# Four transformer layers on one core: narrow attentions turn queries and keys by DMA, weight loads and buffer releases change places

## What is computed

```python
x = x + L0_xattn(layernorm(x), ctx)   # narrow: 32 heads of 16, 8 key heads, rotary positions
x = x + L0_ffn(layernorm(x))          # 512 -> 1792 -> 512, gated by silu
x = x + L1_xattn(layernorm(x), ctx)   # wide: 32 heads of 128, keys = context + latents, rms norms
x = x + L1_ffn(layernorm(x))          # 8 experts of rank 16, two picked
x = x + L2_xattn(layernorm(x), ctx)   # narrow, no rotary positions
x = x + L2_ffn(layernorm(x))          # 8 experts 512 x 512, two picked
x = x + L3_xattn(layernorm(x), ctx)   # wide, keys = context, additive mask
x = x + L3_ffn(layernorm(x))          # base 512 x 512 and 16 experts of rank 64

# one attention
scores = einsum('bhqd,bhkd->bhqk', q, k) * scale
probs = softmax(scores)
ctx_out = einsum('bhqk,bhkd->bhqd', probs, v)
return ctx_out @ Wo
```

## Time and profile before

| | before |
|---|---|
| median of 3 runs | 2209.41 us (2207.28 to 2210.55) |
| profiled execution | 2211.04 us, its span 2209.2 us |
| PE busy | 2017.0 us (91%) |
| DVE busy | 1607.9 us (73%) |
| ACT busy | 1350.0 us (61%) |
| POOL busy | 206.2 us (9%) |
| DMA, dynamic queue | 142.51 MB, 27.4% of 16 engines' span |

### The profile page before, as it was taken

How to read it: one execution, slowest core, us unless ns; L and a number is a source line. 1 busy time by engine, 2 the same in 40 slices (tenths; PEclk the granted TensorE clock), 3 DMA queues, 4 the chain that set the end, 5 groups by cost and what they waited for, 6 DMA issues and landing times.

```text
span 2209.2 us, 40607 instructions
## 1 busy us (share of the span) xinstructions
PE 2017.0 (91%) x14240; PEld 1161.3 (53%) x14240; DVE 1607.9 (73%) x4139; ACT 1350.0 (61%) x3913; POOL 206.2 (9%) x211
## 2 busy tenths in 40 slices
PE   3898999999999999999975798999899999999788
PEld 2554444465655666666643455444455555555444
DVE  6676555676767777777768667766788888888873
ACT  3665212287777777777753566333688888888621
POOL 3664000000000000000000354000000000000010
PEclk8999999999999999999998999999999999999989
DMA  4000111224444444444440000111133433343200
GB/s 194 21 11 2 58 58 39 77 58 87 105 80 89 80 106 96 80 89 89 92 87 20 20 20 11 68 39 58 28 90 72 89 88 86 65 90 84 61 5 39
DMA packets 268761, 145.10 MB, mean 66 GB/s; under 512 B 259472, under 2 KB 259472, under 8 KB 261136
## 3 DMA queue, kind: packets, MB, share of 16 engines
q1 hardware_dynamic: 268560, 142.51, 27.4%
HBM read 77.44 MB, written 2.10 MB: 36 GB/s over the span
## 4 chain that ended last, share of the span: by engine, by line
PE 73%; DVE 12%; ACT 6%; DMA 4%; issue 4%; POOL 1%; SPq 0%; ACTq 0%; DVEq 0%; POOLq 0%
PE bank L659 67%; DMA pT<-hid 3%; ACT hid L1608 2%; PE bank L770 1%; DVE hid L2220 1%; PE bank L1048 1%; DVE xnT_lo L1793 1%; DVE wa_lo L1726 1%; PE bank L786 1%; PE bank L787 1%; ACT probs L1567 1%; DVE xn L1782 1%; DVE stats L1749 1%; DVE negmax_n L1909 1%; DVE bd_lo L1922 0%
## 5 line engine op out<-in xcount | busy, mean ns | idle before, releaser
L659 PE MATMUL bank<-xnT_hi,wa_hi 128*128 128x512 f16 x736 | 279.8, 380 | 4.5 <-PE bank L659 2.6
L659 PE MATMUL bank<-xnT_lo,wa_hi 128*128 128x512 f16 x736 | 279.7, 380 | 0.0
L659 PE MATMUL bank<-xnT_hi,wa_lo 128*128 128x512 f16 x736 | 279.5, 380 | 0.0
L659 PE MATMUL bank<-wo_hi,oT_hi 128*128 128x512 f16 x576 | 219.9, 382 | 27.7 <-DVE oT_lo L2210 26.7
L2220 DVE SCALAR_TENSOR_TENSOR hid<-probs,inv_total,hid 128x256 f16<-128x256 f32 (+1 forms) x512 | 180.0, 413 | 81.5 <-ACT hid L1608 81.5
L659 PE MATMUL bank<-wo_hi,oT_lo 128*128 128x512 f16 x576 | 219.9, 382 | 0.0
L659 PE MATMUL bank<-wo_lo,oT_hi 128*128 128x512 f16 x576 | 219.9, 382 | 0.0
L659 PE MATMUL bank<-wa_hi,xnT_hi 128*128 128x512 f16 (+3 forms) x640 | 203.7, 324 | 5.5 <-DVE xnT_lo L1793 2.2
L659 PE MATMUL bank<-wa_lo,xnT_hi 128*128 128x512 f16 (+3 forms) x640 | 203.7, 324 | 0.0
L659 PE MATMUL bank<-wa_hi,xnT_lo 128*128 128x512 f16 (+3 forms) x640 | 203.5, 323 | 0.0
L1567 ACT ACTIVATE probs<-bank,negmax,rms_r 128x256 f32<-128x256 f32 x256 | 141.2, 561 | 98.5 <-DVE negmax L2176 98.5
(11 more groups left out here) (260 smaller groups left out, 4973.4 us busy)
## 6 DMA issues: line engine op xcount, KB each, us to landing
raw<-in_w_qkv_dram SPq DMA_DIRECT2D x18, 1536.0 KB, 7.0
raw<-in_w_out_dram SPq DMA_DIRECT2D x18, 1024.0 KB, 5.4
raw<-in_w_ffn_dram SPq DMA_DIRECT2D x15, 1024.0 KB, 4.9
pT<-hid SPq DMA_TRANSPOSE x256, 3.1
raw<-in_w_ffn0d_dram SPq DMA_DIRECT2D x7, 512.0 KB, 3.7
x<-in_x_dram SPq DMA_DIRECT2D x4, 512.0 KB, 5.4
expert_b<-in_expert_b_dram SPq DMA_DIRECT2D x1, 2048.0 KB, 9.5
kT<-k SPq DMA_TRANSPOSE x128, 2.4
```

The lines of the kernel that those rows point to most:

```text
L659: mm = pe.matmul(dst, l, r, start=start and k == 0, stop=stop and k == n - 1)
```

## The change

1. **Narrow attentions.** `turn_q`, `turn_k`, `q_rows` and `k_rows` are gone from PE, ACT and DVE. `turn_narrow(n, b)` on SP issues two transposing DMAs a tile: all 16 blocks of `q_parts` into `qst`, and eight blocks of `k_parts` into `kst`. For the latter `k_parts` is laid out twice as wide (128 x 1024), with the zero blocks in it, so that the turned tile is block-diagonal at once; POOL clears `k_parts` instead of `kst`. `proj_q(b)` on PE waits for the reader of bank Q in place of `nb_kst`. ACT and DVE refill the parts once the DMA has landed.
2. **SP's order.** The loads that stood ahead of each narrow attention are now issued between its tiles (`NARROW_LOADS`) or after them. In the wide stages the loads due in step s stand between `turn_probs(s)` and `turn_keys(s + 2)`, in both layers.
3. **Releases.** In the wide stages the wait and release of `qkv_used` move behind `project_q`, those of `out_used` into the next step behind `project_kv`. In the experts of layer 2 the release moves behind the first matmuls of the next expert; in the feed-forward of layer 0 it moves ahead by one down-projection.

```diff
+            def turn_narrow(n, b):
+
+                BB = n * B + b
+                if b == 0:
+                    sp.wait_ge(n_consts, n + 1)
+                if b >= 2:
+                    sp.wait_ge(ng_turned, (BB - 1) * G)
+                sp.wait_ge(nb_qparts if n == 0 else nb_qlo, b + 1)
+                sp.dma_start_transpose(qst_turned[:, b % 2], q_parts[:, :]).then_inc(nb_qturned, 16)
+                sp.wait_ge(nb_kparts if n == 0 else nb_klo, b + 1)
+                sp.dma_start_transpose(kst_turned[:, b % 2], k_parts[:, :]).then_inc(nb_kturned, 16)
+
+            def narrow(n, last):
+
+                for b in range(B):
+                    turn_narrow(n, b)
+                    if b in NARROW_LOADS[n]:
+                        load_item(NARROW_LOADS[n][b])
+                for k in range(max(NARROW_LOADS[n].values()) + 1, last):
+                    load_item(k)
...
             for n in range(2):
+                narrow(n, FIRST_LOAD[n])
                 turn_keys(n, 0)
                 turn_keys(n, 1)
                 for s in range(UNITS):
                     turn_probs(n, s)
+                    for k in wide_loads(n, s):
+                        load_item(k)
                     if s < UNITS - 2:
                         turn_keys(n, s + 2)
-                    for k in wide_loads(n, s):
-                        load_item(k)
...
-                pool.memset(bd_flat[:, 0:2048], 0.0)
+                pool.memset(k_parts[:, :], 0.0).then_inc(nb_kzero, 1)
...
                     if e == 0:
-                        pe.wait_ge(nb_kst, BB + 1)
-                        pe.wait_ge(nb_qst_b, BB + 1)
+                        pe.wait_ge(nb_vlo, BB + 1)
+                        pe.wait_ge(nb_qturned, 16 * (BB + 1))
+                        pe.wait_ge(nb_kturned, 16 * (BB + 1))
...
-                    if g == 1 and f < B:
-                        turn_q(f, 0)
-                    if g == 2 and f < B:
-                        turn_q(f, 1)
-                        turn_k(f)
...
+                    done = s - LATE[n] - 2
+                    if done >= 0 and done % B == B - 1 and done < UNITS - 1:
+                        pe.wait_ge(w_out, n * UNITS + done + 1)
+                        pe.sem_inc(out_used, 1)
...
+                    if s + 5 < UNITS:
+                        project_q(U, s)
                     if s < UNITS - 2 and (s + 2) % B == B - 1:
                         pe.wait_ge(w_kvproj, U + 3)
                         pe.sem_inc(qkv_used, 1)
-                    if s + 5 < UNITS:
-                        project_q(U, s)
...
-                    if r % B == B - 1:
-                        pe.wait_ge(e_y, r + 1)
+                    if r % B == 0:
+                        pe.wait_ge(e_y, r)
                         pe.sem_inc(qkv_used, 1)
```

More of the change, by code:

```diff
@@ L190 @@
 FIRST_LOAD = [min(t) for t in WIDE_LOADS]
+NARROW_LOADS = [{b: NUMBER[item] + 2 for item, b in t.items()} for t in (
+    {("w_out0", 0): 2, ("w_ffn0", 0): 4}, {("w_out2", 0): 2, ("w_ffn2", 0): 4})]
 def wide_loads(n, s):
@@ L319, in p_turned_part @@
             return pT_flat[:, at:at + HPG * S]
-        k_parts = squares[:, 0:256].bitcast(F16)
-        q_part_slots, k_part_slots = (t.rearrange("p (c m s d) -> p s m c d", m=2, s=4, d=ND) for t in (q_parts, k_parts))
+        k_parts = squares[:, 0:512].bitcast(F16)
+        q_part_slots = q_parts.rearrange("p (c m s d) -> p s m c d", m=2, s=4, d=ND)
+        k_part_slots = k_parts.rearrange("p (c u s d) -> p s u c d", u=4, s=4, d=ND)[:, :, 0:4:3]
         def v_heads(t):
@@ L530, in turn_keys @@
                                        k16[:, u % 2, 0:runs * P]).then_inc(w_kturned[u % 2], 16)
+            for k in range(1, min(NARROW_LOADS[0].values())):
+                load_item(k)
+                if k == 2:
+                    sp.dma_start(expert_b[:, :, :], ins["expert_b"]).then_inc(expert_b_loaded, 16)
+                    sp.dma_start(wgate2[:, :], ins["wgate2"]).then_inc(wgate2_loaded, 16)
             for n in range(2):
+                narrow(n, FIRST_LOAD[n])
                 turn_keys(n, 0)
@@ L536, in _ @@
                     turn_probs(n, s)
+                    for k in wide_loads(n, s):
+                        load_item(k)
                     if s < UNITS - 2:
                         turn_keys(n, s + 2)
-                    for k in wide_loads(n, s):
-                        load_item(k)
                 if n == 0:
-                    for k in range(FIRST_LOAD[0] + len(WIDE_LOADS[0]), FIRST_LOAD[1]):
+                    for k in range(FIRST_LOAD[0] + len(WIDE_LOADS[0]), min(NARROW_LOADS[1].values())):
                         load_item(k)
@@ L724, in proj_kv @@
                         pe.sem_inc(qkv_used, 1)
[L726 to L751, removed]
                 def scores(b, e):
@@ L1226, in ffn2 @@
                     expert(48 + 2 * b)
+                    if b == 0:
+                        pe.wait_ge(e_y, 48)
+                        pe.sem_inc(qkv_used, 1)
                     if b >= 3:
@@ L1362, in k_part @@
                     if b:
-                        act.wait_ge(nb_turn_k, BB)
+                        act.wait_ge(nb_kturned, 16 * BB)
+                    else:
+                        act.wait_ge(nb_kzero, n + 1)
                     if rope:
@@ L1425, in narrow @@
                         k_part(f)
-                    if g == 1 and f < B:
-                        q_rows(f)
                     if g == 6 and f < B:
@@ L1911, in row_max @@
                                       negate=True).then_inc(ng_max, 1)
-                def k_rows(b):
-                    BB = n * B + b
-                    dve.wait_ge(nb_turn_k, BB + 1)
-                    if b == 0:
-                        dve.wait_ge(n_consts, n + 1)
-                    if b >= 2:
-                        dve.wait_ge(ng_turned, (BB - 1) * G)
-                    for m in range(2):
-                        half = slice(m * 64, (m + 1) * 64)
-                        op = dve.tensor_copy(kst[half, b % 2, :, m, :], halves16(Q)[half, 0:512].rearrange("p (c t) -> p c t", c=4))
-                    op.then_inc(nb_kst, 1)
                 def spread_max(b):
@@ L1966, in narrow @@
                         add(b - 2)
-                    if g == 2 and f < B:
-                        q_rows(f)
-                        k_rows(f)
                     if g == 2 and b >= 1:
```

50 lines of the change are left out of this document (17 added, 33 removed).

## The result

The changed kernel takes 2237.17 us in the median of 4 runs (2230.45 to 2241.26), the kernel before 2208.85 (4 runs, 2207.28 to 2210.55): a ratio of 1.0125, 95% interval 1.0112 to 1.0138, or 28.3 us slower. 2235 was predicted.

A forecast was written before the change was run, and what follows sets the result against it. PE was taken to set the end nearly everywhere (its matmuls 67% of the chain of waits). -20 + 31 + 5 - 6 + 9 + 4 + 3 = +26 on 2211.0 gave 2237, median 2235 us; range 2197 to 2260.

The forecast's parts named there:

- Part 1: Layer 1: loads moved ahead of the keys' turn end PE's waits for turned probabilities, -20 us (15 to 22).
- their cover: Layer 1: turned keys land some 2 us before the scores that read them, so nothing is late next.
- the first term: Layer 1: all 18.5 us of PE's 14 waits for `pT` go, besides the half-clock stretches.
- Part 2: Layer 3: keys queued behind loads make scores late, +31 us, plus 5 for the clock behind large loads.
- the turned keys come 0.6 to 1.6 us later, I take 1.1: Layer 3: keys land 1.1 us after their load, making scores 3.0 us late behind large loads, 1.4 behind smaller.
- Part 3: Moved releases: PE's waits for its own matmuls shrink, -6 us (3 to 7); 2.6 us in `down_proj` stay.
- Part 4: Layer 0 narrow attention: two DMAs replace PE's transposes and lengthen the loop, +9 us, and +4 for the clock.
- the 9 us term: Layer 0 narrow attention: DMA latency starts scores 1.05 to 1.65 us later a tile, 9 us over 7 tiles (5 to 13).
- the clock term: Layer 0 narrow attention: four tiles instead of two have a half-clock stretch, +4 us (-4 to +11).
- Rival C: Narrow tiles and layer 3's large loads: clock falls in nearly every new stall, about +25, 2260 us; chance 0.1.
- Part 5: Layer 2 narrow attention: DMA takes as long as what it replaces, +0.1 a tile, first tile +2; +3 us (0 to 6).
- The sum: Whole kernel: all predicted gains and costs together, +26 us, giving 2235 us; chance 0.6.

The follow-up runs named there:

- best version: The kernel before with only the layer-1 loads ahead of the keys' turn and the moved releases: 2181.65 us, 0.9884 of the kernel before.
- the filler: The changed kernel with 13 constant matmuls a tile (7 in layer 2) before the wait for turned halves, except first tiles: 2217.18 us, 1.0045 of the kernel before.

## Why the prediction was right, and where its terms were not

The forecast of 2235 us is 2.2 below the result, and the kernel is slower by far more than 0.2%, which had 0.73. The signs of all parts held, and so did their mechanisms. But two terms were off by 8 and 12 us, in opposite directions. That the forecast came within 2.2 us is luck; that it came out some 30 us slower is not.

| part | predicted | measured alone | between the changed kernel and one without it |
|---|---|---|---|
| layer-1 loads | -20 | -17.0 | |
| layer-3 loads | +31 and +5 | +27.7 | +27.5 |
| releases | -6 | -5.8 | |
| narrow attentions | +9, +4 and +3 | +28.9 | +28.0 (best version against it) |

**Part 1, layer-1 loads (-20, bounds 15 to 22).** Right in mechanism; the keys had their cover and nothing was late next (10.60 to 10.62 us in the steps from 530 to 1114 us). Mis-sized was the first term: 18.5 us took in every wait of the window for `pT`, where 14.1 were due to loads. A group's sum must be cut to the cases with the cause, and the view of `pT` after the edit shows that 4.4 us in 3 waits never had it.

**Part 2, layer-3 loads (+36, bounds 24 to 49).** Right in sign and in what waits: PE's weight loads stand for `kT` behind 14 of the 15 loads, longer behind the large ones (2.26 to 3.97 us) than behind the small (0.44 to 1.12), and its matmuls behind 11. The failed step is "the turned keys come 0.6 to 1.6 us later, I take 1.1". They came 0.2 to 0.6 us behind the load in 13 of the 15 cases (1654.30 to 1654.63, 1619.8 to 1620.3), 0.8 in one and 1.2 in one. With the layer-3 loads alone there was more scatter: 0.3 to 0.6 in eleven, 1.0 to 2.0 in four. Both rows of the estimate were turns of the probabilities, issued three microseconds after their load and twice as large as the keys' turn. With some 0.4 in the place of 1.1, a small load costs 0.7 and not 1.4, and a large one, with a landing of 6.7 instead of 7.0, about 2.0 and not 3.0 (PE stood for 1.77 to 2.41 us in five of them and 3.48 in one). The small ones carried most of the error: 4.6 us in sum against 13. The large ones came to 20.5 against 18 + 5, three of six with the clock at half behind them, as predicted; one of these, 14.47 us long, is the dearest single step (6.5 us) and nearly balances the shorter stalls. The rule of the Trainium skill that the prediction set against this part (DMA: Bandwidth & Descriptors, Rules for kernel authors: issue early, wait late) held in layer 1, where it was worth 17.0 us, and for the transfer behind the load in layer 3 it did not, at 27.7.

**Part 3, releases (-6, bounds 3 to 7).** Right. The six waits of `down_proj` stayed, as predicted, but at 0.30 us each and not 0.44, so 7.6 us of waits went and not 6.8.

**Part 4, narrow attention of layer 0 (+9 and +4).** The latency was right: the estimate of 4.5 us for the turn of 16 blocks met 4.3 to 4.4, the keys' landing behind the queries' 1.2 us, and the period with the clock held the predicted one: 135.3 us for seven tiles, where 18.9 to 19.5 each make 132 to 137. Against the kernel before that is the upper end of the 9 us term, for its 128.8 us hold about 5 of half clock in two tiles (20.6 and 20.0 us against 17.8), so the latency cost about 11 or 12, inside the bounds. The failed step is the clock term: "Two of the present tiles have a stretch at half clock and take 20.0 instead of 17.8 us; with such stalls I expect four: +4". It was seven of seven. Net of the two it had, layer 0 lost about 6 us more to the clock, not 4; the larger part of the error is the 4.7 us of layer 2 below, for which no term stood. A stall of 2.6 to 3.6 us is about as long as the one of the earlier trace rows, which was the case that I had at hand and which had cost the clock; I counted it for half of the tiles without a row that shows a stall of that length passing without loss. The windows behind the seven scores lack 4 x (1 - clock) each, 12.4 us in sum, and the filler gives 11.4 back. Rival C, the clock falling in nearly every new stall, is what happened in layer 0; it fell in three of seven tiles of layer 2 and behind three of the six large loads.

**Part 5, narrow attention of layer 2 (+3).** The latency was right again, 3.3 us against 3.2 from DVE to the scores. No clock term stood here; but PE, which no longer has the transposes, stands 1.67 to 2.30 us in each tile, and in three of the seven the clock fell behind that (0.63, 0.60 and 0.58 over the next 4 us; over the whole stretch 0.95 against 1.00). These three took 19.1, 19.2 and 19.2 us; the tile of 19.0 had its full clock and took 18.8 before. That is the 4.7 us that the filler returns. I had said of this loop that the DMA takes as long as what it replaces, which is so, and had not asked what PE does meanwhile: before, it was transposing, and the clock stayed at 1.00 in all seven tiles.

**The sum.** With the parts as measured alone it would be 33.8 instead of 26; together the parts gave 28.3. What is left of the narrow edit once the clock is held is 28 - 20 = 8 us: by traces 6.5 in the tiles of layer 0, -0.3 in those of layer 2 and 2.2 in the two first tiles. That is the DMA's latency against PE's transposes, less the 5 us or so of half clock in the kernel before, which the one with the filler doesn't have. Nor do the runs show why stalls of like length differ: behind the large loads the clock fell after stalls of 2.14, 2.41 and 3.48 us and not after 1.77, 1.90 and 2.28, and in layer 2 it fell after one stall of 1.67 us and one of 1.69 and not after others of 1.68 and 1.70. In layer 0 of the kernel before it fell twice with no such stall at all: ahead of the scores of 82.48 and 120.35, which begin at half clock, PE's waits were 0.99, 0.47 and 0.47 us and 0.88 and 0.52. So the length of one stall does not decide it, and what does is open.

## What to carry to other kernels

Ask of each transfer not only whether it is issued early, but what it puts behind itself on its queue and how long until the reader of that: the same swap was worth 17 us where the reader came late, cost 28 where it had 6.66 us, and cost nothing once half the bytes stood ahead. Work taken off TensorE is only a gain if TensorE has something else to do in that place; here it stood still in place of its transposes, and the DMAs that took them over cost 28 us, of which 20 came back when that time was filled. Price a new stall with the clock that falls behind it in every case where a stall of that length has been seen to do so, and look for a counterexample before counting fewer; but short waits close together can cost the clock too, as two tiles of the kernel before show.

## What the runs showed of the hardware

- The granted clock fell behind each of seven stalls of 2.6 to 3.6 us in layer 0 (0.50 to 0.61 over the next 4 us), and stayed at 0.99 when 2.97 us of each stall were filled with matmuls of a constant, which, with 7 matmuls a tile in layer 2, gave back 20.0 us in all. In the kernel before it fell in two tiles of layer 0 in which no wait ahead of it was above 0.99 us.
- A turn of 16 blocks from memory on the chip to memory on the chip landed 4.3 to 4.4 us after its issue in the median (4.2 to 6.1 over all) and kept SP for 1.3 to 2.1 us; eight blocks landed in 3.1, two in 2.3. The growth is 0.13 to 0.15 us a block.
- A turn of two blocks issued right behind a load of 1024 or 1536 KB landed 0.2 to 0.6 us after it in 13 of 15 cases of the changed kernel, in the others 0.8 and 1.2; with the layer-3 loads alone in four cases 1.0 to 2.0.
- PE waited 0.3 to 0.5 us for its own last matmul at a release. Taking 7.6 us of such waits away brought 5.8 us, with an interval of about 3 on either side.
